# SiLU of the second MLP as a tanh on ScalarE and two products on VectorE, in a four-layer cross-attention kernel

## What is computed

```python
def mlp(x, wg, wu, wd):
    return jax.nn.silu(x @ wg) * (x @ wu) @ wd      # 256 -> 1024 -> 256
...
hn = rmsnorm(h, mlp_norm_w)
h = residual + mlp(hn, w_gate, w_up, w_down)
```

## Time and profile before

| what | value |
|---|---|
| median of 3 runs | 3233.84 us (3232.46 to 3250.25) |
| profiled execution, its own time | 3241.35 us |
| its span, first to last instruction | 3239.5 us |
| mean granted TensorE clock | 0.863 |
| PE busy | 2702.2 us (83%) |
| PEld busy | 1954.3 us (60%) |
| DVE busy | 1863.5 us (58%) |
| ACT busy | 1481.2 us (46%) |
| POOL busy | 684.0 us (21%) |

### The profile page before, as it was taken

One profiled execution on the slowest core, in us unless ns is written; L12 is line 12 of the kernel. 1 busy time (PEld: TensorE's weight loads), 2 busy tenths in 40 slices (PEclk: granted clock), 3 DMA queues, 4 the chain that ended last, 5 costly groups with the idle time before them and its releaser, 6 DMA issues. The chain is left out here.

```text
span 3239.5 us, 52743 instructions
## 1 busy us (share of the span) xinstructions
PE 2702.2 (83%) x19640; PEld 1954.3 (60%) x19640; DVE 1863.5 (58%) x4255; ACT 1481.2 (46%) x3426; POOL 684.0 (21%) x872
## 2 busy tenths in 40 slices
PE   4789888989898899898989889889888774447997
PEld 3567666766666667676767667667666552334443
DVE  4964668575666566756675757576654420004676
ACT  3754356454454544444554535464443211224564
POOL 2410122121211111211211211122111000004775
PEclk9799899989897979797989899999897865558999
DMA  4000000000000000000000000000000001001110
GB/s 174 2 2 1 10 9 3 9 2 9 2 9 2 9 2 9 2 9 2 9 2 9 2 9 2 10 1 8 1 5 1 5 0 39 0 0 32 31 36 24
DMA packets 19675, 40.46 MB, mean 12 GB/s; under 512 B 2528, under 2 KB 10032, under 8 KB 18672
## 3 DMA queue, kind: packets, MB, share of 16 engines
q1 hardware_dynamic: 12976, 17.32, 1.9%
q10 hardware_dynamic: 6464, 19.93, 1.6%
HBM read 27.80 MB, written 9.44 MB: 11 GB/s over the span
## 5 line engine op out<-in xcount | busy, mean ns | idle before, releaser
L955 PE MATMUL psum<-hT,w_l 128*128 128x256 f32 x2048 | 488.9, 396 | 13.5 <-ACT hT L1277 8.7
L955 PEld LDWEIGHTS psum<-hT,w_l 128*128 128x128 f32 x2048 | 400.3, 199 | 87.7 <-issue 16.8
L682 POOL TENSOR_TENSOR rstd<-ms,half 128x2 f32<-128x2 f32 (+1 forms) x144 | 100.2, 696 | 1198.2 <-DVE ms L1042 810.3
L1375 ACT ACTIVATE work<-psum 128x1024 f32<-128x1024 f32 (+1 forms) x224 | 221.0, 1022 | 278.8 <-PE psum L880 227.8
L1359 ACT ACTIVATE work<-psum,nbias,qs 128x256 f32<-128x256 f32 x512 | 282.6, 573 | 46.5 <-DVE nbias L1145 44.8
L1391 ACT ACTIVATE work<-psum,offset 128x1024 bf16<-128x1024 uint16 (+1 forms) x192 | 210.2, 1117 | 188.2 <-PE psum L892 157.6
L773 PE MATMUL psum<-hT,w_l 128*128 128x256 f32 x896 | 241.7, 422 | 15.2 <-ACT hT L1277 12.9
L1277 ACT ACTIVATE hT<-psum,cols 128x256 f32<-128x256 f32 x256 | 122.2, 532 | 244.7 <-PE psum L764 244.2
L722 POOL TENSOR_SCALAR work<-work 128x1024 f32<-128x1024 f32 x128 | 135.1, 1055 | 459.4 <-DVE work L1212 446.4
L967 PE MATMUL psum<-w_l,work 128*128 128x256 f32 x1024 | 227.9, 381 | 1.6 <-DVE work L1235 1.0
L1189 DVE RECIPROCAL work<-psum 128x256 f32<-128x256 f32 x96 | 168.3, 1753 | 94.9 <-PE psum L932 94.8
(11 more groups left out here) (178 smaller groups left out, 4995.9 us busy)
## 6 DMA issues: line engine op xcount, KB each, us to landing
w_l<-in_w_l ACTq DMA_DIRECT2D x1, 5120.0 KB, 24.4
x_res<-in_x SPq DMA_DIRECT2D x16, 256.0 KB, 2.7
res<-x_res ACTq DMA_DIRECT2D x16, 256.0 KB, 2.3
w_l<-res SPq DMA_DIRECT2D x16, 256.0 KB, 2.8
out<-w_l ACTq DMA_DIRECT2D x16, 256.0 KB, 2.0
w_l<-in_w_l ACTq DMA_DIRECT2D x1, 3072.0 KB, 12.7
w_l<-in_w_l SPq DMA_DIRECT2D x2, 1024.0 KB, 8.6
w_l<-in_w_l ACTq DMA_DIRECT2D x2, 1024.0 KB, 16.1
```

Source lines behind the costliest of these rows:

```text
L955: mm = eng.matmul(banks.tile(key)[:, h * TOKENS:(h + 1) * TOKENS], w1[:, k, h, m * P:(m + 1) * P], hT[p][:, k, :], start=(k == 0), stop=(k ...
L1375: eng.activation(pt(n, p)[0:a.kp, :], banks.pair(key)[0:a.kp, :, :].rearrange("p r n -> p (r n)"), ACT.Exp) \
```

## The change

SiLU is written by way of the hyperbolic tangent: silu(g) = 0.5 g (1 + tanh(g / 2)). ACT computes the tangent; a first DVE instruction adds 1 and multiplies by g, which it reads from the gate half of the bank, back into the gate tile; DVE waits for its own signal `gated`; a second DVE instruction multiplies by 0.5 and by the up half. The plan's cost of the DVE task goes from 0.4 to 0.45 for the first MLP and to 1.0 for the second. The SiLU of the scan stays as it is.

```diff
@@ plan(), mlp
-            acts.append(work.add("vector", "hidden", name, m, p, 0.4, g, *acts[-1:]))
+            acts.append(work.add("vector", "hidden", name, m, p, 0.45 if name == "geglu" else 1.0, g, *acts[-1:]))
@@ vector, hidden
-                        ins = eng.tensor_tensor(actT(p)[:, m, :], banks.tile(key)[:, TOKENS:2 * TOKENS], gate(m, p), ALU.mult)
+                        eng.scalar_tensor_tensor(out=gate(m, p), in0=gate(m, p), scalar=1.0, in1=banks.tile(key)[:, 0:TOKENS],
+                                                 op0=ALU.add, op1=ALU.mult).then_inc(*gated.next((name, m, p)))
+                        eng.wait_ge(*gated.at((name, m, p)))
+                        ins = eng.scalar_tensor_tensor(out=actT(p)[:, m, :], in0=gate(m, p), scalar=0.5,
+                                                       in1=banks.tile(key)[:, TOKENS:2 * TOKENS], op0=ALU.mult, op1=ALU.mult)
@@ scalar, hidden
-                        ins = eng.activation(gate(m, p), banks.tile(key)[:, 0:TOKENS], ACT.Silu)
+                        ins = eng.activation(gate(m, p), banks.tile(key)[:, 0:TOKENS], ACT.Tanh, scale=0.5)
```

More of the change, by code:

```diff
@@ L598, in build @@
         act_ready = sig("act_ready")
+        gated = sig("gated")
         uT_ready = sig("uT_ready")
```

## The result

The changed kernel takes 3214.62 us (median of 8 runs, 3202.09 to 3223.49), the kernel before 3233.9 us in the same comparison. The ratio is 0.9939, 95% interval [0.9914, 0.9963]: 0.6% faster, 20 us.

The account below looks back on a forecast made before the run. PE was taken to bound the main stage, busy 86%. Loads -5, pairs +3.5 and the end's order -5 gave about -7 us, so 3233.84 - 7 = 3227 us, range 3194 to 3261.

Parts of the forecast that it names:

- the forecast's own range: Whole kernel: a time of 3214 to 3243 us, given a chance of 0.48.
- The counts and the unit costs: Main stage: 52 table loads for 94, tanh at 385 ns, each half of the pair at 482 ns.
- The loads, -5 us: Main stage: 42 table loads fewer on ACT, of which four places where PE stood still give back 5 us.
- The pair, +3.5 us: Second MLP's gate product on DVE: six PE waits each 0.58 us longer, 3.5 us; bounds 0 and 74 us.
- The new order, -5 us: Main stage's end, where PE starves with only round 15 left: fewer matmuls there, -5 us taken between 0 and -15.
- my bound: Between the last matmuls of rounds 14 and 15: at most 15 us saved by matmuls moved ahead.
- The clock: Main stage, rival: new order brings three more slow stretches at 1.2 GHz, +33 us, 3260 us; chance 0.14.
- two fewer: Main stage: two slow stretches at 1.2 GHz fewer in the new order would give 3205 us.
- The spreading relief: Main stage, rival: half of ACT's 53.9 us counts, 27 us, 3205 us; chance 0.28, shared with a luckier order.
- The late pairs: Main stage, rival: 40% of the pairs' 74 us of DVE reach PE, 3253 us; chance 0.08.

Follow-up runs that it names:

- Experiment 3: Kernel before, its order kept, with the tangent of half the gate in place of SiLU and one product: 0.9961, 3224.4 us.
- experiment 4: Kernel before, its order and SiLU kept, with the pair of DVE instructions in place of the one product: 1.0019, 3243.66 us.
- experiment 1: Changed kernel with the plan's old costs (0.4 for both MLPs), so in the order of before: 0.9981, 3231.43 us.
- experiment 8: Changed kernel with plan costs 0.4 for the first MLP and 1.0 for the second: 0.9893, 3205.43 us.
- experiment 12: Changed kernel, costs 0.45 and 1.0 kept, with a plan adding 4.0 us to ACT tasks that need another table: 1.0051.
- experiment 2: Kernel before (SiLU, one product) with the plan's costs 0.45 and 1.0, so in the changed order: 1.005, 3253.38 us.
- experiment 6: Kernel before with the plan's costs 0.45 and 1.0, SiLU kept, the pair in place of the one product: 1.0033.

## Why the prediction was right, and where it was not

The forecast was 3227 us, the range 3194 to 3261; the time was 3214.6. It lies in the range and at the lower edge of the forecast's own range, but the gain of 0.6% is over the bound of 0.5%, a case that I had given 0.30, with 0.50 for no change. I had the sum at -7 and it was -20. That it came so near is partly luck: the largest part of the gain came from the clock, which my sum held still. By its steps:

**The counts and the unit costs held, but for one.** 52 loads in the main stage and none at the tangent; 385 ns for the tangent; ACT busy 1209.72 us there, where I had 1212. The pair was mis-sized: I took 482 ns for each half from L1235, whose scalar comes from an SBUF column; the two of the pair, with immediate scalars, take 420 ns, much as the plain product. The added DVE time was 52 us, not 74.

**The loads, -5 us: the places were right, the term was not the whole.** Experiment 3 has the order of before, so the same four instructions can be found in it. The earlier trace rows showed PE waiting 1.27, 1.87, 1.36 and 3.56 us there. With the loads gone the waits of 1.27 and 1.36 us are no longer there, and the other two are these:

```profile
1060.33 0.39 PE L828 MATMUL psum<-work 32*128 32x256 bf16 x4 [1.12 <-ACT work L1359]
...
1867.72 1.01 PE L854 MATMUL psum<-kc,work 32*128 32x77 f32 x14 [2.13 <-ACT work L1326]
```

That is 1.27 + 0.75 + 1.36 + 1.43 = 4.8 us where I had 5, and PE's idle time over the main stage fell by 5.9 us (375.2 to 369.2 in the next row), its waits for ACT by 5.1 of them. The two profiled executions are 16 us apart, and the other 10 us are in the busy time:

```profile
0.00:2680.00 2680.00, 2310.77 (x17773) 1736.61 (x17774) 1665.35 (x3727) 1211.27 (x2488) 482.01 (x536) 0.89 0.03 11
```

As much lies at one place, the stretch about the slow one of the earlier trace rows. The same 900 or so matmuls in the same order, in the kernel before and then in experiment 3:

```profile
1095.00:1237.00 142.00, 128.29 (x896) 94.83 (x895) 80.83 (x181) 62.91 (x114) 23.42 (x26) 0.83 0.02 6
```

```profile
1094.00:1226.00 132.00, 118.08 (x898) 89.99 (x897) 80.44 (x181) 56.43 (x109) 23.43 (x26) 0.91 0.02 7
```

10 us shorter, with PE busy 10.2 us less: the stretch at 1.2 GHz from 1165.50 to 1196.00 us is down to 10 us. But this isn't what the loads did. In experiment 4, which has the same order of PE and all its loads, and in experiment 1 these matmuls also have one slow stretch of 10.2 us there, and take 133 and 134 us in place of 142. The other executions agree: the mean clock was 0.8665 over the 12 of experiment 3 and 0.8660 over the 35 of the kernel before beside them, while the two that were profiled had 0.866 and 0.863. So the clock hardly moved with the loads in this order, and the profiled execution of the kernel before was one of its slower ones. Of the 12.6 us, whose interval is 7 to 18, the traces explain about 6, as idle time; the rest stays open.

**The pair, +3.5 us.** Measured +6 [1, 11] in the first order, nothing to be seen in the changed one. The kind is right. I had six waits that grow by 0.58 us each; experiment 4 has 12 waits, 8 us more in all, so the pair also made waits that were not there.

**The new order, -5 us: the sign right, the size and the mechanism too small.** Its share was -14 us with the tangent (and +16 with SiLU, by way of its loads). I had read only the program's end, and there the bound holds in full. From the last matmuls of round 14 to those of round 15, before and after:

```profile
2536.08 1.08 PE L976 MATMUL psum<-hT,wb 128*64 128x256 f32 x4 [1.11 <-ACT hT L1277]
...
2681.09 1.97 PE L976 MATMUL psum<-hT,wb 128*64 128x256 f32 x4 [1.11 <-ACT hT L1277]
```

```profile
2531.11 1.97 PE L977 MATMUL psum<-hT,wb 128*64 128x256 f32 x4
...
2661.13 1.97 PE L977 MATMUL psum<-hT,wb 128*64 128x256 f32 x4 [1.11 <-ACT hT L1283]
```

145.0 us before, 130.0 after: the full 15 us of my bound. I had kept only a third of it since the moved work lands in the stretch ahead. It did land there, 17132 matmuls in the trace up to that point for 17056 (float32 matmuls stand twice in a trace: the two of `drive` in the lists are four rows in it), and that stretch still ended 5 us earlier:

```profile
0.00:2536.00 2536.00, 2214.83 (x17056) 1665.90 (x17056) 1616.08 (x3636) 1232.30 (x2478) 472.67 (x528) 0.89 0.03 11
```

```profile
0.00:2531.00 2531.00, 2195.87 (x17132) 1662.69 (x17132) 1671.01 (x3766) 1184.46 (x2449) 473.64 (x529) 0.91 0.03 11
```

PE did 76 matmuls more there in 19 us less of busy time, at a granted clock of 0.91 for 0.89. Nor is the program's end a guide to an order's worth. From the last matmuls of round 14 to those of round 15 it is 160.0 us in experiment 8, 15 longer than before, and that kernel is 1.1% faster than the one before; it is 115.4 us in experiment 12, which is 0.5% slower.

**The rivals.** The clock was one of mine, with the wrong sign in front: I priced three slow stretches more at +33 us, and gave "two fewer" half a sentence and 3205. What I wrote would show it, PE's busy time moving with the clock, is what the profile shows, and experiment 2 has it without the tangent. The spreading relief would be worth 27 us in the first order; it was 12.6, and at most 18, so it is refuted there. In the changed order it has its size, 30 to 36 us, and its sign, 21 us less of PE's waits for ACT, but for 55 loads. That a plan which interleaves the functions more has more of its loads on the path fits both orders, and stays a guess from two. The late pairs: half of the sign that I named for them came, since PE's waits for DVE grew by 24 us. But with one product in the same order they are 197.3 us (experiment 2), and with the pair in the first order 179.2 (experiment 4), where the kernel before has 171.1. So it is the order that made them longer; the pair adds 8 us in the first order and 2 in the changed one (199.6 in experiment 6), and L1241 and L1244 released no wait of PE in the changed kernel. The failed step is thus the one that priced the order by its tail alone, at -5 us, and let the clock stand still; the order was worth -14 us with the tangent, 26 us less of busy time against 10 more of idle time.

**The length of a load.** No set of removed loads in one order gave more than 0.66 us for each, below the 1.28 us of the row. By the 2.66 us that the Trainium skill gives in ScalarE: Activation LUTs, section What ACT_TABLE_LOAD costs, one load on the path would cost twice the row; no run here shows such a cost.

## What to carry to other kernels

Where a list scheduler at build time sets the order, an edit that also changes one of its costs is two changes: time the edit in the old order and the new order without the edit, since here the order moved the time by up to 1.7% and the edit by 0.2 to 1.1%. Count what a removed instruction is worth by the waits of the bounding engine behind it, not by its own length, and do not then optimise the count: the two kernels with 20 table loads fewer were 1.1 and 1.2% slower than the changed one. And for the engine that bounds the stage, split the difference into idle and busy time first; if the busy time of the same instructions moved, look at the clock, and look at it in every execution on record: here one profile of the kernel before made 10 us of clock look like the gain of an edit.

## What the runs showed of the hardware

- A DVE instruction with a scalar and two tensors of 128x256 float32, one of them in PSUM, takes 420 ns in the pair, with an immediate scalar, and 482 ns at L1235, with the scalar in an SBUF column. So it isn't the kind of instruction that makes it slow. L1235 also has its other inputs the other way round (the first in PSUM), and no run sets the two apart. A dependent second instruction of the pair starts 0.03 us behind the first:

```profile
2604.97 0.42 DVE L1241 SCALAR_TENSOR_TENSOR work<-work,psum 128x256 f32<-128x256 f32 x1 [6.33 <-ACT work L1418]
2605.42 0.42 DVE L1244 SCALAR_TENSOR_TENSOR work<-work,psum 128x256 f32<-128x256 f32 x1
```

- The tangent needed no load in any place, behind exponentials or behind GELU (128 tangents in the changed kernel, 48 of them with a GELU as the last other function).
- The granted clock depends on small things. The same matmuls in the same order had 0.83 in the profiled execution of the kernel before and 0.91 in that of experiment 3, and over the main stage PE's busy time for the same work lay between 2276.64 us (experiment 8) and 2320.85 us (the kernel before). These are single executions, but the means over all executions, 0.877 and 0.8655, say the same. What about an order keeps the clock up stays open: the runs show that it does, not why.
- Executions of one kernel differ by up to 1.0% (3216.89 to 3250.25 us over all of the kernel before), as much as most effects measured here; only ratios over several runs could tell the parts apart.
